# Sixteen small exponents per tile in place of one wide one: the window softmax of a six-layer local attention

## The reference, cut to what matters

```python
def attn_layer(x, Wqkv, qs, ksc, Wo):
    ...
    q = l2norm(q) * qs
    k = l2norm(k) * ksc
    ...
    q = q * cos * scale + rotate_half(q) * sin * scale
    inv = 1.0 / scale
    k = k * cos * inv + rotate_half(k) * sin * inv
    out = local_attention(q, k, v)
    ...
# in local_attention; QK_SCALE is 8.0
sim = jnp.einsum('bhwie,bhwje->bhwij', bq, bk2) * QK_SCALE
sim = jnp.where(mask, -jnp.finfo(sim.dtype).max, sim)
attn = jax.nn.softmax(sim, -1)
out = jnp.einsum('bhwij,bhwje->bhwie', attn, bv2)
```

## Time and profile before

| | |
|---|---|
| median of 3 runs | 3234.56 us (3229.79 to 3239.2) |
| profiled execution, its own time | 3241.93 us |
| its span in the trace | 3239.9 us |
| PE, DVE, ACT, POOL busy over the span | 75%, 70%, 50%, 49% |
| first and last subtraction of the stack (L1365) | at 543.2 and 2464.9 us |

### The profile page before, as it was taken

How to read it: one execution, slowest core, us unless ns; L and a number is a source line. 1 busy time by engine, 2 the same in 40 slices (tenths; PEclk the granted TensorE clock), 3 DMA queues, 4 the chain that set the end, 5 groups by cost and what they waited for, 6 DMA issues and landing times.

```text
span 3239.9 us, 59830 instructions
## 1 busy us (share of the span) xinstructions
PE 2443.0 (75%) x23988; PEld 1434.5 (44%) x23988; DVE 2273.8 (70%) x1982; ACT 1629.6 (50%) x1731; POOL 1575.7 (49%) x1678
## 2 busy tenths in 40 slices
PE   2857674788898988898888888888987375767253
PEld 1212122556566655565555555556655121211153
DVE  2765447998888888888888888888884276445301
ACT  1524443566666666666666666666664142444110
POOL 0000005777777777777777777777772000000202
PEclk7888897999999999999999999999999587889577
DMA  4001100000000000000000000000000100110122
GB/s 147 20 23 42 42 1 2 15 1 15 2 2 23 11 6 2 23 7 9 2 23 5 11 2 23 4 12 2 8 2 1 42 20 23 42 55 1 29 68 66
DMA packets 59866, 67.16 MB, mean 21 GB/s; under 512 B 12550, under 2 KB 50308, under 8 KB 57796
## 3 DMA queue, kind: packets, MB, share of 16 engines
q1 hardware_dynamic: 57460, 58.63, 6.2%
q0 software_dynamic: 2128, 4.72, 0.6%
HBM read 46.04 MB, written 17.56 MB: 20 GB/s over the span
## 4 chain that ended last, share of the span: by engine, by line
PE 25%; DVE 21%; POOL 19%; issue 19%; ACT 9%; DMA 5%; SPq 1%; POOLq 1%; DVEq 0%; ACTq 0%; PEldq 0%
DVE big L1276 6%; POOL small L504 6%; DMA pxs<-part_rows 4%; POOL small L505 4%; DVE small L1332 3%; ACT big L1049 3%; DVE big L1354 3%; PE bank L795 3%; PE bank L713 3%; ACT big L1078 2%; PE bank L838 2%; POOL big L515 2%; DVE small L1333 2%; ACT pxs L1104 2%; POOL small L507 2%
## 5 line engine op out<-in xcount | busy, mean ns | idle before, releaser
L520 POOL TENSOR_TENSOR sc<-sc,small 128x1024 f32<-128x1024 f32 x96 | 263.5, 2744 | 326.4 <-DVE small L1375 326.4
L1354 DVE TENSOR_TENSOR big<-big,small 128x1024 f32<-128x1024 f32 x192 | 385.0, 2005 | 46.6 <-POOL small L507 46.6
L1276 DVE TENSOR_REDUCE big<-bank 128x2 f32<-128x1024 f32 x256 | 292.7, 1214 | 137.0 <-PE bank L627 137.0
L795 PE MATMUL bank<-pxs,mw 128*128 128x256 f32 x1536 | 368.8, 384 | 0.0
L713 PE MATMUL bank<-wqk,xs 128*128 128x512 f32 x768 | 351.3, 601 | 20.7 <-ACT xs L1065 20.7
L627 PE MATMUL bank<-pxs 128*128 128x512 bf16 x512 | 166.7, 427 | 235.1 <-DMA pxs<-part_rows 145.9
L795 PEld LDWEIGHTS bank<-pxs,mw 128*128 128x128 f32 x1536 | 292.4, 193 | 100.6 <-issue 69.0
L1332 DVE TENSOR_REDUCE small<-big 128x32 f32<-128x2048 f32 x96 | 219.0, 2281 | 120.0 <-ACT big L1078 119.8
L504 POOL TENSOR_TENSOR small<-small 128x32 f32<-128x32 f32 x288 | 242.6, 843 | 37.7 <-DVE small L1334 22.7
L555 POOL DMA_INDIRECT dispatch_rows<-sc,qks x16 | 15.5, 972 | 504.3 <-DVE qks L1523 499.8
L1049 ACT ACTIVATE big<-bank 128x1024 f32<-128x1024 f32 x256 | 247.2, 1022 | 9.8 <-PE bank L659 6.7
(11 more groups left out here) (206 smaller groups left out, 5047.9 us busy)
## 6 DMA issues: line engine op xcount, KB each, us to landing
pxs<-part_rows SPq DMA_DIRECT2D x32, 448.0 KB
part_rows<-big SPq DMA_DIRECT2D x96, 128.0 KB
wqk<-in_L_ffn_w SPq DMA_DIRECT2D x32, 256.0 KB, 3.0
wqk<-in_L_ffn_Wqkv SPq DMA_DIRECT2D x12, 512.0 KB, 4.3
wvt<-in_wv_layers_t SPq DMA_DIRECT2D x6, 512.0 KB, 4.7
wol<-in_L_ffn_Wo SPq DMA_DIRECT2D x6, 512.0 KB, 5.7
w<-in_L_ffn_W SPq DMA_DIRECT2D x6, 341.0 KB
dispatch_rows<-pxs SPq DMA_DIRECT2D x5, 256.0 KB, 6.6
```

Of the source, the lines that this page charges most:

```text
L520: pool.tensor_tensor(p3, p3, rden(i).unsqueeze(2).broadcast_to([P, LH, 64]), ALU.mult).then_inc(l_pn, 1)
L795: m = pe.matmul(bank[:, 6, part * 2 * P:(part + 1) * 2 * P], mw[:, 2 * (a % 4) + s, a // 4, :], pxs[:, part, a, s, :], start=(a == 0 and s ...
L1276: dve.tensor_reduce(nm[:, qt, 2 * p:2 * p + 2], bank[:, 2 * (u % 3):2 * (u % 3) + 2, :], AX.X, ALU.max, negate=True).then_inc(a_mx, 1)
L1354: dve.tensor_tensor(r3, r3, nrm(i)[:, half * LH:(half + 1) * LH].unsqueeze(2).broadcast_to([P, LH, LD]), ALU.mult).then_inc((l_yq, l_yk)[h ...
```

## The change

`exponentials` no longer reads the subtracted scores from SBUF. It reads each head's 64 scores from PSUM in an instruction of its own, with the negated maximum of that head as bias (one value per partition), writes the exponents to SBUF and takes their sum from ScalarE's accumulator (`accum_out`). VectorE's maximum now comes out negated and is kept for two tiles in turn; its subtraction and its sum go. The factor 8 moves into the constant tables for the queries. TensorE's `weigh`, which writes over the scores' banks, waits for the last of the 16 exponents where it waited for the subtraction.

```diff
             def turn_windows(T, b, i):
                 if isinstance(T, int) and T == 0:
-                    pe.wait_ge(l_e, 1)
+                    pe.wait_ge(l_p, LH)
...
                     pe.wait_ge(l_pe, T)
-                    pe.wait_ge(l_e, T + 1)
+                    pe.wait_ge(l_p, LH * (T + 1))
                     weigh(T - 1, i + 3, 0)
...
             def exponentials(T, i):
+
                 act.wait_ge(l_e, T + 1)
-                act.activation(probs(i), probs(i), ACT.Exp, scale=8.0).then_inc(l_p, 1)
+                if not (isinstance(T, int) and T < 2):
+                    act.wait_ge(l_pt, T - 1)
+                settle(act)
+                for h in range(LH):
+                    act.activation(probs(i)[:, h * 64:(h + 1) * 64], bank[:, 4 + h // 8, (h % 8) * 64:(h % 8 + 1) * 64], ACT.Exp,
+                                   bias=small[:, 1, (i % 2) * LH + h:(i % 2) * LH + h + 1],
+                                   accum_out=small[:, 5, (i % 2) * LH + h:(i % 2) * LH + h + 1]).then_inc(l_p, 1)
...
             def softmax(T, i):
                 dve.wait_ge(l_s, T + 1)
                 s3 = bank[:, 4:6, :].rearrange("p a (h j) -> p (a h) j", j=64)
-                dve.tensor_reduce(u_mx, s3, AX.X, ALU.max).then_inc(l_mx, 1)
-                dve.wait_ge(l_mx, T + 1)
                 if not (isinstance(T, int) and T < 2):
-                    dve.wait_ge(l_pt, T - 1)
-                settle(dve)
-                dve.tensor_tensor(probs(i).rearrange("p (h j) -> p h j", j=64), s3,
-                                  u_mx.unsqueeze(2).broadcast_to([P, LH, 64]), ALU.subtract).then_inc(l_e, 1)
+                    dve.wait_ge(l_p, LH * (T - 1))
+                    settle(dve)
+                dve.tensor_reduce(small[:, 1, (i % 2) * LH:(i % 2 + 1) * LH], s3, AX.X, ALU.max, negate=True).then_inc(l_e, 1)
 
             def sums(T, i):
-                dve.wait_ge(l_p, T + 1)
-                dve.tensor_reduce(u_den, probs(i).rearrange("p (h j) -> p h j", j=64), AX.X, ALU.add).then_inc(l_dn, 1)
-                dve.wait_ge(l_dn, T + 1)
+                dve.wait_ge(l_p, LH * (T + 1))
                 if not (isinstance(T, int) and T < 2):
                     dve.wait_ge(l_pn, T - 1)
                 settle(dve)
-                dve.reciprocal(rden(i), u_den).then_inc(l_rd, 1)
+                dve.reciprocal(rden(i), small[:, 5, (i % 2) * LH:(i % 2 + 1) * LH]).then_inc(l_rd, 1)
...
-        for s in (scale, 1.0 / scale):
+        for s in (8.0 * scale, 1.0 / scale):
```

More of the change, by code:

```diff
@@ L242, in build @@
         l_tk, l_tq, l_kd, l_qe, l_kh = (sem(n) for n in ("l_tk", "l_tq", "l_kd", "l_qe", "l_kh"))
-        l_s, l_mx, l_e, l_p, l_dn, l_rd, l_pn, l_pt, l_pe = (
-            sem(n) for n in ("l_s", "l_mx", "l_e", "l_p", "l_dn", "l_rd", "l_pn", "l_pt", "l_pe"))
+        l_s, l_e, l_p, l_rd, l_pn, l_pt, l_pe = (
+            sem(n) for n in ("l_s", "l_e", "l_p", "l_rd", "l_pn", "l_pt", "l_pe"))
         l_xt, l_xe, l_px, l_pc, l_mm, l_mw, l_m, l_res, l_xf, l_fn = (
@@ L1322, in _ @@
             GUESS = float(0x5F3759DF - 0x40400000)
-            ss, u_mx, u_den = small[:, 0, :], small[:, 1, 0:LH], small[:, 5, 0:LH]
+            ss = small[:, 0, :]
             def square_sums(T, i):
```

## The result

The changed kernel takes 3259.91 us (median of 5 runs, 3258.04 to 3266.39) against 3229.79 for the kernel before beside it. The ratio is 1.0092, 95% interval 1.0072 to 1.0113: 30 us slower. The forecast was 3380, 146 us slower.

The account below looks back on a forecast made before the run. No engine was full; a loop from ScalarE's squares through VectorE and back was taken to bound each slot. Four slots of 86.6 us against 80.5 gave +146 us over 24 iterations, so 3380 us, range 3200 to 3490.

Parts of the forecast that it names:

- c: Start-to-start price of one of ScalarE's new per-head exponents with its sum, taken as 0.39 us.
- the fixed 174 ns in full: Cost of fetching a head's sum on ScalarE, taken as the width-independent 174 ns without overlap, giving c = 0.39 us.
- the second of my four bounds: Sum's fetch on ScalarE costs the fixed 174 ns with 100 ns overlapped, giving c = 0.29 us.
- rival 2: Cheap fetch of the sum on ScalarE: c = 0.27 to 0.32, -30 to +45 us, 3205 to 3280; chance 0.18.
- my own slope: Each 0.01 us of c moves all four slots of an iteration: 16 x 96 x 0.01 = 15 us.
- The turning point: Length of ScalarE's exponent block where the change neither gains nor loses: 4.8 us, c = 0.29 us.
- E: ScalarE's block of 16 exponents plus 0.1 us hop from VectorE: 6.3 us, where subtraction and exponent took 2.5.
- my four sums: Slots 0 to 3, squares to squares: head, E, 3.6 us of copies; 21.3, 24.6, 20.3, 20.4, together 86.6 against 80.5.
- "Slower": Forecast sign for the whole kernel: slower than the kernel before, chance 0.74, against 0.20 faster and 0.06 same.
- The loop: ScalarE's squares start VectorE's work up to the maximum, then ScalarE's exponents, copies and next squares; 80.5 us per four slots.
- VectorE's part: Subtraction and sum removed from VectorE: 2.8 us a slot, 269 us if VectorE alone bound; 1.4 us off ahead of the exponent.
- rival 4: TensorE's clock falls to 0.76 as its busy share drops in the stack: +250 us, 3485; chance 0.05.

Follow-up runs that it names:

- runs 5 and 6: ScalarE's squares moved between the two halves of the weighed copies, in the changed kernel (3257.45 us, ratio 1.0085) and in the kernel before (3231.62 us, ratio 0.9998).
- Runs 8 and 9: Changed kernel with the first projections copy ahead of the exponents (3372.09 us); changed kernel with a one-column exponent bringing the table load earlier in slots 0 and 1 (3189.38 us).
- run 4: Changed kernel with one 1,024-column exponent from PSUM in place of the 16, without maximum subtraction or sum: 3140.83 us, ratio 0.9711 to the kernel before.
- run 2: Changed kernel with the sum back on VectorE and 16 exponents without accumulator output: 3249.95 us, ratio 1.0038 to the kernel before.
- run 3: Changed kernel with every head's exponent split into two instructions of 32 columns, each with accumulator output: 3722.59 us, ratio 1.1495 to the kernel before.
- run 8: Changed kernel with the first copy of the projections ahead of the 16 exponents: 3372.09 us, ratio 1.0429 to the kernel before.

## Why the prediction was wrong, point by point

**The term that failed: c.** My sum took 0.39 us for a head, "the fixed 174 ns in full", because "the value depends on the instruction just ahead, so I don't let it overlap". The trace has 0.29: 0.20 for the exponent (I had 0.22) and 0.09 for the read, which does overlap (I had 0.17 in full). That is the second of my four bounds and the case of rival 2, whose 3205 to 3280 hold the result. The block was 4.6 us and not 6.3. The step that chose between bounds chose by an argument about dependence and not by a row, and it was worth 16 x 96 x 0.10 = 154 us by my own slope.

**The slope.** I put 15 us on each 0.01 us of c, a price of 1 for each microsecond of the block. Measured it is 0.66 below 4.6 us and 1.24 above. At 6.3 us the kernel would by this price (an estimate, 96 x 1.7 x 1.24) have been some 200 us over the measured one, 230 over the kernel before, where I had 146. So the sum was too low for its own block. The turning point lies between 3.2 and 4.6 us (ratios 0.98 and 1.0092; a straight line crosses 1 at 4.2, c = 0.26), where I had 4.8 and 0.29.

**The slots, and the sign.** With E = 4.6 my four sums would be 19.6, 22.9, 18.6 and 18.7, together 79.8, which is 0.7 under 80.5: the kernel would have been 17 us faster, near 3218. Measured are 21.3, 23.3, 19.4 and 18.5, together 82.6, and it is 30 us slower. So the right c brings the time near and turns the direction. "Slower" came true because a price too high for the read covered what the sum lacks elsewhere, and that is luck.

Slots 1 and 3 hold, slot 2 is 0.8 too short and slot 0 is 1.7 too short. In slot 0 the reason is that I had laid out one iteration for all. A layer has four iterations. In slot 0 of one of them ScalarE copies the second half of the new layer's mixing weights (L1137) ahead of the keys, and in slot 0 of the next the program's loop ends. The iteration of the earlier trace rows is neither. Means over iterations 6 to 21, from the starts of the squares, us:

```
                             slot 0              whole iteration
                           before  changed       before  changed
no seam (two of four)       17.7    19.7          81.2    81.5
weights' copy in slot 0     19.7    24.1          80.9    85.1
loop's end in slot 0        19.7    23.4          81.8    85.0
```

Without a seam slot 0 is what my sum gives, 19.7 for 19.6, and its first exponent comes 11.4 us after the squares as I had it (12.1 in the iteration shown above). With a seam it comes after 14.2 to 16.5 us. Nearly all that the changed kernel loses, it loses in the two iterations with a seam. At the one with the weights' copy TensorE waited for that copy and then for the exponents, and worked at the lower clock behind both waits:

```profile
1596.49 1.09 PE L739 MATMUL bank<-ident,big 128*128 128x128 f32 x8 [2.77 <-ACT mw L1137]
1597.42 3.31 PE L795 MATMUL bank<-pxs,mw 128*128 128x256 f32 x8
...
1611.13 3.58 PE L787 MATMUL bank<-sc,xnw 64*128 64x256 f32 x16 [2.10 <-ACT sc L1100]
```

The same two products take 1.89 and 2.00 us in this slot of the kernel before, where `weigh` waited for nothing; the granted clock there is 1.00 (1582.7 to 1604 us) and here 0.86 (1591 to 1616 us). At the loop's end TensorE stood 3.22, 4.30, 2.95 and 4.46 us with nothing to wait for in the trace, where it was 2.03, 2.26, 3.17 and 3.11 in the kernel before, and behind it worked at the lower clock (1.97 for 1.09 us):

```profile
1346.63 1.97 PE L724 MATMUL bank<-ident,big 128*128 128x128 f32 x8 [4.30 <-issue]
1348.38 1.92 PE L739 MATMUL bank<-ident,big 128*128 128x128 f32 x8
```

All this is read from the traces and was not tested by a run of its own. Why the seams cost more in the changed kernel, the wait for a ScalarE that has more in its queue or the clock behind it, stays open.

**The loop.** I named the loop from the squares through VectorE. Its members all grew as I wrote, and VectorE waited for the squares, but runs 5 and 6 show that shortening it by a reordering gives nothing. Runs 8 and 9 show the path in slots 0 and 1: ScalarE's queue from one block to the next, with its waits for TensorE. Without a seam my sums still held there, because block and copies are in both. This was right by luck of overlap, not by reading.

**VectorE's part.** "Worth something only where VectorE itself is late (slots 1 and 2)": slot 2 fell by 2.3 us as forecast (21.7 to 19.4, I had 20.3 with the longer block). The size of both together is 94 us (run 4, with the wide exponent's other reads and waits in it). That the subtraction's removal lengthens the wait for GpSimd is in the trace: VectorE stood 2.20 us ahead of the query scaling in slot 3 of the iteration shown, where 0.8 us had lain between the subtraction and GpSimd's next start. That the sum lies beside other work was wrong: it costs 77 us behind a block of 3.2 (run 2).

**The clock** (rival 4) did not fall over the stack at this size, 0.98 as before, though it did in single slots at the seams. In run 3 it was 0.89.

## What to carry to other kernels

Before costing a split into many small instructions, get the distance between the starts, not the durations, and for a step without any row leave the choice between bounds open in the forecast, not only in the range. Test a loop by moving a member out of it: here two orders of the same queue gave the same time, and taking a load out of the queue gave 76 us. Lay out every kind of iteration, not one: here the quiet ones were level and those at a layer's seams lost. Put the corrected term back into the sum and look at the sign, before the direction is counted as a hit. When a change fills an engine's queue, look at what else stands ahead of the filled place; a table load that had been hidden came to stand on the path, and one instruction in idle time took 76 us off.

## What the runs showed of the hardware

The accumulator's read is a record of its own on ScalarE. In a row of such pairs the recorded durations grow over the 16 heads (303 ns the shortest and 410 the longest exponent of all, 192 and 305 the reads), while the starts stay 0.29 us apart, so the growing durations cost nothing. After idle times of 5.14 and 3.83 us on TensorE `weigh` and the product behind it ran wholly or partly at the lower clock: 3.79 and 2.07 us in run 3 (granted clock 0.50 there) and 3.26 and 1.51 us in run 8, for 2.14 and 1.12 in the changed kernel. The wait just ahead does not tell it alone: after 1.24 us `weigh` took 2.14, and after 2.10 us it took 2.14 in the changed kernel at 1363.05 us and 3.58 at 1611.13, behind a slot with the wait of 2.77 us in it.
